# Routing's small SBUF operations move from VectorE to GpSimd in a fused attention and mixture-of-experts kernel

## The reference

```python
x = x + _L0_xcond_ref(_layernorm(x), ctx, ctx, lengths)      # 8 heads
x = x + _L0_ffn_ref(_layernorm(x), gate_w, w1, w2, w3)

scores = jnp.einsum('ti,ei->te', xt, gate_w)                 # 2048 tokens, 8 experts
probs = jax.nn.softmax(scores, axis=-1)
expert_weights, expert_indices = jax.lax.top_k(probs, 2)
expert_weights = expert_weights / expert_weights.sum(axis=-1, keepdims=True)
x1 = jax.nn.silu(jnp.einsum('ti,eoi->teo', xt, w1))          # 512 -> 1024
x3 = jnp.einsum('ti,eoi->teo', xt, w3)
expert_outs_all = jnp.einsum('teo,eio->tei', x1 * x3, w2)    # 1024 -> 512
```

## Time and profile before

| | us |
|---|---|
| median of three runs | 1231.14 (1230.88 to 1231.62) |
| the profiled execution | 1232.27 |
| its span, first to last instruction | 1230.7 |
| POOL's prep of slot 2 to prep of slot 13 | 331.50 |
| mean granted TensorE clock | 0.951 |

### The profile page before, as it was taken

One profiled execution on the slowest core, in us unless ns is written; L12 is line 12 of the kernel. 1 busy time (PEld: TensorE's weight loads), 2 busy tenths in 40 slices (PEclk: granted clock), 3 DMA queues, 4 the chain that ended last, 5 costly groups with the idle time before them and its releaser, 6 DMA issues.

```text
span 1230.7 us, 19877 instructions
## 1 busy us (share of the span) xinstructions
PE 1035.8 (84%) x5081; PEld 413.9 (34%) x5082; DVE 810.9 (66%) x953; ACT 410.7 (33%) x734; POOL 638.4 (52%) x578
## 2 busy tenths in 40 slices
PE   1799988999998998832999999999999999999910
PEld 0123322333333333211444444444444444444400
DVE  5877877888888887213853954938677395953354
ACT  3266666666666676721111111111100111011100
POOL 6454766676767762322841834807566182830055
PEclk9699999999999999975999999999999999999965
DMA  6465655565555552105875756647666575753387
GB/s 175 153 223 150 186 153 175 174 189 181 175 177 181 179 150 70 48 27 161 203 141 143 185 132 171 171 96 212 153 197 176 147 191 149 191 133 86 71 227 257
DMA packets 212839, 195.58 MB, mean 159 GB/s; under 512 B 137376, under 2 KB 176288, under 8 KB 207392
## 3 DMA queue, kind: packets, MB, share of 16 engines
q1 hardware_dynamic: 198624, 123.80, 38.5%
q0 software_dynamic: 14176, 71.31, 17.7%
HBM read 111.44 MB, written 52.95 MB: 134 GB/s over the span
## 4 chain that ended last, share of the span: by engine, by line
PE 49%; POOL 20%; DMA 11%; issue 10%; DVE 7%; POOLq 2%; ACT 1%; SPq 1%; DVEq 0%
PE rows L1072 23%; PE heads_out L1072 12%; POOL W L423 7%; PE heads_out L989 4%; PE scores L976 4%; DVE nm L717 3%; PE rows L962 3%; DMA rb<-recips_dram 3%; POOL W L422 3%; DMA recips_dram<-rden 2%; DMA U<-wpack_dram 2%; POOL us L500 1%; POOL us L497 1%; PE misc L1039 1%; POOL U L422 1%
## 5 line engine op out<-in xcount | busy, mean ns | idle before, releaser
L1072 PE MATMUL rows<-W,U 128*128 (+1 forms) x1776 | 391.9, 381 | 23.6 <-DMA U<-stage 19.5
L717 DVE TENSOR_REDUCE nm<-rows 128x2 f32<-128x1024 f32 x256 | 304.2, 1216 | 61.2 <-PE rows L962 53.1
L598 ACT ACTIVATE W<-scores 128x512 f32<-128x512 f32 x512 | 283.9, 596 | 153.0 <-PE scores L976 151.7
L1072 PEld LDWEIGHTS rows<-W,U 128*128 128x128 bf16 x1776 | 174.3, 98 | 236.0 <-issue 30.4
L663 ACT ACTIVATE U<-rows 128x512 f32<-128x512 f32 x78 | 46.4, 597 | 520.3 <-PE rows L1072 511.5
L962 PE MATMUL rows<-W,U 96*128 96x512 bf16 x512 | 151.6, 400 | 71.0 <-DVE nm L717 43.6
L1072 PE MATMUL heads_out<-W,U 128*128 x888 | 199.4, 381 | 13.3 <-issue 10.6
L423 POOL TENSOR_TENSOR W<-U,W 128x2048 bf16<-128x2048 f32 x42 | 172.6, 4110 | 7.7 <-POOL W L422 7.7
L900 DVE TENSOR_TENSOR U<-rows,U 128x512 f32<-128x512 f32 x78 | 53.6, 687 | 183.6 <-ACT U L663 183.5
L976 PE MATMUL scores<-U,W 128*128 128x512 bf16 x512 | 168.1, 386 | 5.6 <-ACT W L598 4.7
L907 DVE TENSOR_TENSOR U<-U 128x512 bf16<-128x512 f32 x78 | 162.7, 2086 | 2.7
(11 more groups left out here) (146 smaller groups left out, 676.4 us busy)
## 6 DMA issues: line engine op xcount, KB each, us to landing
U<-wpack_dram POOLq DMA_DIRECT2D x42, 1024.0 KB, 5.8
parts_dram<-U SPq DMA_DIRECT2D x32, 384.0 KB, 3.9
U<-parts_dram SPq DMA_DIRECT2D x32, 384.0 KB, 3.9
W<-parts_dram SPq DMA_DIRECT2D x32, 384.0 KB, 5.0
stage<-slots_dram SPq DMA_DIRECT2D x39, 256.0 KB, 2.8
expert_out_dram<-U SPq DMA_DIRECT2D x39, 256.0 KB
parts_dram<-U SPq DMA_DIRECT2D x32, 256.0 KB, 4.0
stage<-wpack_dram POOLq DMA_DIRECT2D x12, 512.0 KB, 4.8
```

The lines of the kernel that those rows point to most:

```text
L598: s.activation(probs[:, w % 2, j, kk, :], sc[u % 2][:, :], ACT.Exp) \
L717: v.tensor_reduce(nm[:, bb.parity, 2 * k:2 * k + 2], p1[k % 2][:, :].rearrange("p (c k) -> p c k", c=2), AX_X, ALU.max, negate=True).then_ ...
L1072: ins = m.matmul(bank, part_of(s_part, k), W[:, bass.ds(at_w, 512)], start=(k == 0 and n == 0), stop=(k == n_chunks - 1 and n == 2))
```

## The change

DVE keeps three routing operations, those that read PSUM: the maximum and its index (L729, L731 before) and the sum of rank and first rows (L767 before). The others go to POOL in two groups, in steps of their own. Group A (six steps) stands between prep and the weight chunk: two copies, where the expert numbers now pass through a new tile `order_f`, a cast and a copy; two compares with a scalar column in place of one with a broadcast; the sum of the masks. Group B (six steps) stands between the keys and the scatters: the product; a sum over the eight experts as three halving additions in place of one reduction; the cast to `idx`; and the running sum of masks, now last. DVE waits before it overwrites `sorted8` or `place` until POOL has read the last ones, and the table operations wait for the last `idx_ready`.

```diff
@@ -16,7 +16,7 @@
 P = 128
 LOOP_FIRST, LOOP_LAST = 2, 6
 LEAD = 4
-ENGINE_STEPS = {"prep": 10, "keys": 4, "z": 4, "route_a": 6, "route_b": 5}
+ENGINE_STEPS = {"prep": 10, "keys": 4, "z": 4, "top": 2, "route_a": 6, "route_b": 6}
 
 
 class Batch:
@@ -149,6 +149,7 @@
         ltri = sb("ltri", [P, P], BF16)
         onesb = sb("onesb", [P, P], BF16)
         idx = sb("idx", [P, 2, 2], I32)
+        order_f = sb("order_f", [P, 2], F32)
 
         tio_i = sb("tio_i", [P, T + 1], I32)
         tio = sb("tio", [P, 2, T + 1], F32)
@@ -190,7 +191,7 @@
 
 
         names = """setup numbered consts rows_set gate_in len_in ln_ready sb_ready table_chain
-            prep_steps keys_steps first_keys z_steps route_a_steps route_b_steps queries_out keys_out
+            prep_steps keys_steps first_keys z_steps top_steps route_a_steps route_b_steps queries_out keys_out
             sums_out rec_out m_out den_in rec_in m_in cv_in p1_ready p1_used scores_ready exp_done pv_done
             og_ready vt_ps vt_ready u_ready us_ready t_ready x1_ready x1_kept zt_ps zt_ready
             gate_ready gate_used mask_ready rank_ready rank_used idx_ready rec_ready st1_steps
@@ -454,6 +455,23 @@
                     g.nop().then_inc(S["prep_done"], 1)
                     if b.within(-2, -2):
                         constants()
+                pv2 = b.plus(-2)
+                if pv2.within(0, B - 1):
+                    a_steps = Steps(hold, S["route_a_steps"], pv2.n, ENGINE_STEPS["route_a"])
+                    hold(S["gate_used"], b.n - 1)
+                    if pv2.within(1, B - 1):
+                        hold(S["rank_ready"], b.n - 2)
+                    two = experts2[:, bass.ds(pv2.n, 1), :].rearrange("p o a -> p (o a)")
+                    a_steps.step(g.tensor_copy(scores2[:, bass.ds(pv2.n, 1), :].rearrange("p o a -> p (o a)"),
+                                               sorted8[:, 0:2]))
+                    a_steps.step(g.tensor_copy(order_f[:, :], order8[:, 0:2]))
+                    a_steps.step(g.tensor_copy(two, order_f[:, :]))
+                    for a in range(2):
+                        a_steps.step(g.tensor_scalar(masks[:, a, :], numbers[:, :], order_f[:, a:a + 1], None,
+                                                     ALU.is_equal))
+                    a_steps.step(g.tensor_tensor(maskb[:, :], masks[:, 0, :], masks[:, 1, :], ALU.add))
+                    a_steps.end()
+                    g.nop().then_inc(S["mask_ready"], 1)
                 if b.within(1, 1):
                     for n in range(2):
                         pool.dma_start(stage[:, n, :], wpack[0, :, n * CH:(n + 1) * CH]).then_inc(w_in[n], 16)
@@ -477,9 +495,22 @@
                     high_low(st, pt[:, 3, :], None, cin[:, lb.parity, :], rest[:, :])
                     high_low(st, pt[:, 4, :], pt[:, 5, :], rest[:, :])
                     st.end()
-                pv2 = b.plus(-2)
                 if pv2.within(0, B - 1):
-                    hold(S["idx_ready"], b.n - 1)
+                    b_steps = Steps(hold, S["route_b_steps"], pv2.n, ENGINE_STEPS["route_b"])
+                    row = rows[:, bass.ds(pv2.n, 1), :].rearrange("p o a -> p (o a)")
+                    hold(S["rank_used"], b.n - 1)
+                    b_steps.step(g.tensor_tensor(place[:, 0:2, :], masks[:, :, :],
+                                                 place[:, 2, :].unsqueeze(1).to_broadcast([P, 2, E]), ALU.mult))
+                    for n in (4, 2):
+                        b_steps.step(g.tensor_tensor(place[:, 0:2, 0:n], place[:, 0:2, 0:n], place[:, 0:2, n:2 * n],
+                                                     ALU.add))
+                    b_steps.step(g.tensor_tensor(row.unsqueeze(2), place[:, 0:2, 0:1], place[:, 0:2, 1:2], ALU.add))
+                    if b.within(4, B + 1):
+                        hold(slots_out[pv2.parity], pv2.pair * 32)
+                    b_steps.step(g.tensor_copy(idx[:, b.parity, :], row))
+                    b_steps.step(g.tensor_tensor(mask_sum[:, :], mask_sum[:, :], maskb[:, :], ALU.add))
+                    b_steps.end()
+                    g.nop().then_inc(S["idx_ready"], 1)
                     for a in range(2):
                         pool.indirect_dma_start(
                             out=zs[:, :], out_offset=bass.IndirectOffsetOnAxis(ap=idx[:, b.parity, a:a + 1], axis=0),
@@ -722,25 +753,18 @@
                 maxima(range(0, 2))
                 if routes:
 
-                    a_steps = Steps(dve.wait_ge, S["route_a_steps"], pv2.n, ENGINE_STEPS["route_a"])
+                    tops = Steps(dve.wait_ge, S["top_steps"], pv2.n, ENGINE_STEPS["top"])
                     dve.wait_ge(S["gate_ready"], b.n - 1)
-                    two = experts2[:, bass.ds(pv2.n, 1), :].rearrange("p o a -> p (o a)")
+                    if pv2.within(1, B - 1):
+                        v.nop().then_inc(S["dve_held"], 1)
+                        dve.wait_ge(S["mask_ready"], b.n - 2)
                     v.nop().then_inc(S["dve_held"], 1)
-                    a_steps.step(v.max(sorted8[:, :], misc[:, 0:E]))
+                    tops.step(v.max(sorted8[:, :], misc[:, 0:E]))
                     v.nop().then_inc(S["dve_held"], 1)
-                    a_steps.step(v.max_index(order8[:, :], sorted8[:, :], misc[:, 0:E]))
+                    tops.step(v.max_index(order8[:, :], sorted8[:, :], misc[:, 0:E]))
+                    tops.end()
                     v.nop().then_inc(S["gate_used"], 1)
-                maxima(range(2, 3))
-                if routes:
-                    a_steps.step(v.tensor_copy(scores2[:, bass.ds(pv2.n, 1), :].rearrange("p o a -> p (o a)"),
-                                               sorted8[:, 0:2]))
-                    a_steps.step(v.tensor_copy(two, order8[:, 0:2]))
-                    a_steps.step(v.tensor_tensor(masks[:, :, :], numbers[:, :].unsqueeze(1).to_broadcast([P, 2, E]),
-                                                 two.unsqueeze(2).to_broadcast([P, 2, E]), ALU.is_equal))
-                    a_steps.step(v.tensor_tensor(maskb[:, :], masks[:, 0, :], masks[:, 1, :], ALU.add))
-                    a_steps.end()
-                    v.nop().then_inc(S["mask_ready"], 1)
-                maxima(range(3, 6))
+                maxima(range(2, 6))
                 lb = b.plus(3)
                 if lb.within(0, B - 1):
                     dve.wait_ge(loads[lb.parity], lb.pair * 32 + 32)
@@ -762,23 +786,14 @@
                 maxima(range(7, 8))
                 if routes:
 
-                    b_steps = Steps(dve.wait_ge, S["route_b_steps"], pv2.n, ENGINE_STEPS["route_b"])
                     dve.wait_ge(S["rank_ready"], b.n - 1)
-                    b_steps.step(v.tensor_tensor(place[:, 2, :], misc[:, 0:E], first_rows[:, :], ALU.add))
-                    v.nop().then_inc(S["rank_used"], 1)
-                    b_steps.step(v.tensor_tensor(mask_sum[:, :], mask_sum[:, :], maskb[:, :], ALU.add))
-                    b_steps.step(v.tensor_tensor(place[:, 0:2, :], masks[:, :, :],
-                                                 place[:, 2, :].unsqueeze(1).to_broadcast([P, 2, E]), ALU.mult))
+                    if pv2.within(1, B - 1):
+                        v.nop().then_inc(S["dve_held"], 1)
+                        dve.wait_ge(S["idx_ready"], b.n - 2)
+                    v.nop().then_inc(S["dve_held"], 1)
+                    v.tensor_tensor(place[:, 2, :], misc[:, 0:E], first_rows[:, :], ALU.add) \
+                        .then_inc(S["rank_used"], 1)
                 maxima(range(8, 9))
-                if routes:
-                    row = rows[:, bass.ds(pv2.n, 1), :].rearrange("p o a -> p (o a)")
-                    b_steps.step(v.tensor_reduce(row, place[:, 0:2, :], AX_X, ALU.add))
-                    if b.within(4, B + 1):
-                        dve.wait_ge(slots_out[pv2.parity], pv2.pair * 32)
-                    v.nop().then_inc(S["dve_held"], 1)
-                    b_steps.step(v.tensor_copy(idx[:, b.parity, :], row))
-                    b_steps.end()
-                    v.nop().then_inc(S["idx_ready"], 1)
                 maxima(range(9, 10))
                 if b.within(-3, -3):
 
@@ -828,6 +843,8 @@
             st = Steps(dve.wait_ge, S["table_chain"], 1, 7)
             link = st.step
             dve.wait_ge(S["pv_done"], 4 * B)
+            v.nop().then_inc(S["dve_held"], 1)
+            dve.wait_ge(S["idx_ready"], B)
             link(v.tensor_tensor(gexp[:, :].unsqueeze(2), scores2[:, :, 1:2], scores2[:, :, 0:1], ALU.subtract))
             v.nop().then_inc(S["routed"], 1)
             chosen = experts2[:, :, :].rearrange("p b a -> p (b a)").unsqueeze(2)
```

## The result

The changed kernel takes **1285.32 us** (median of 4 runs, 1283.95 to 1287.34), against 1231.38 (1230.88 to 1240.61) for the kernel before on the same chip. The ratio is 1.0432, 95% interval 1.0401 to 1.0463: 54 us slower. The profiled execution took 1285.01, its span is 1283.6, which is 52.9 more than before.

What follows compares the result with a forecast made beforehand. The prediction took POOL's chain of small dependent operations as the bound in slots 2 to 12. Its terms, 63.8 - 10.9 + 3.7 = +56.6 us, gave 1288.9 on the profiled execution, 1288 against the median; range 1270 to 1308.

Steps and rivals of the forecast that it cites:

- POOL is the period of slots 2 to 12: Attention phase, slots 2 to 12: POOL's chain of small dependent operations sets the 30.1 us slot; PE and DVE follow.
- 5.8 us a slot: Time both groups add to POOL's chain per slot, 2.95 plus 2.85; 63.8 us over slots 2 to 12.
- The `rb` cover of 10.9: Slots 2 to 12: POOL's 10.9 us of waits for the DMA of `rb` all go, leaving +52.9.
- Slots 13 to 16: POOL's slack or idleness hides the added work: 0; at worst +3 in slot 13, +0.5 each in 14 to 16.
- Slot 17: Last slot, nothing hides the groups in its chain: +2.1 for group A, +1.6 for group B, +3.7 together.
- Expert phase 0: Expert phase: none of its instructions changes, so its time changes by 0.
- PE's wait for the mask: Before PE's rank product: group A just ends in time (247.95 against 248.20); a longer wait costs nothing, with 5.8 us spare.
- The first, DVE's relief: Rival, slots 2 to 12: PE and DVE set the period, so relieving DVE makes it faster, 1213 us; chance 0.02.
- The second, the clock: Rival, each slot: PE pauses some 5 us, its clock falls and PE becomes the bound, 1315 us; chance 0.08.
- The third: Rival, slots 2 to 12: the 16.7 us DVE round trip absorbs POOL's work or steps overlap, 1271 us; chance 0.06.

Runs made afterwards that it cites:

- The twelve copies: Kernel before, all routing left on DVE, with POOL repeating both groups' twelve operations on scratch tiles nobody reads: 1284.97 us.
- (10): Kernel before with two DMAs moved, lighter POOL (ACT makes the chunk's high part, prep subtracts the mean directly) and group A on POOL: 1224.92 us.
- B alone: Kernel before with only group B moved to POOL, group A staying on DVE: 1260.99 us.
- A alone: Kernel before with only group A moved to POOL, group B staying on DVE: 1255.02 us.
- (6): Kernel before with SP sending the reciprocals ahead of the key and query reload, and POOL issuing the next chunk's transfer behind z: 1218.64 us.
- (4): Kernel before with the means subtracted directly in prep and z, and the weight chunk's high part made by ACT: 1257.29 us.

## Why the prediction came out as it did

Forecast 1288 in 1270 to 1308; measured 1285.32. By its own steps:

- **POOL is the period of slots 2 to 12: shown.** The twelve copies, with DVE and PE left as they were, give the whole loss.
- **5.8 us a slot: 5.47.** Group A was 2.95 and measured 3.06. A copy or addition takes 0.18 to 0.20, and from one step's start to the next are 0.35 to 0.54, around the 0.40 assumed; the two comparisons with a scalar column take 0.31 to 0.32. Group B was 2.85 and measured 2.55: its steps stand 0.43 apart (2.14 us from the first to the sixth), so that the waits and slices put at 0.45 cost next to nothing. The Trainium skill's factor of two for two-input elementwise work ("GPSIMD Engine Reference", Engine selection) does not show here: L472 takes 0.20, the same addition on DVE 0.17. At this size the wait between two steps costs as much as the step.
- **The `rb` cover of 10.9 goes: 10.6 did.** So the slots gave 60.2 - 10.6 = +49.6 where +52.9 was forecast.
- **Slots 13 to 16 cost nothing: wrong by 4.6.** The term of slot 13 said "0", "at worst +3 if PE comes late itself", and that of slots 14 to 16 "0, at worst +0.5 each". PE did come late. Its clock is 0.67 in the first 5.5 us of slot 14, as the pause in slot 13 left it, and PE starts the transposes of z 2.5 us after z's end (527.01 against 524.48), where it was 0.7 before (475.61 against 474.95). In slot 14 PE is busy 27.65 of 29.73 us; POOL isn't the bound there, so the lost clock shows in full: +3.0, with +1.4 in slot 13. Two other traces bear this out: with the copies and with the change and its DMAs moved slot 14 begins at a granted clock of 1.00, and it takes 27.0 and 27.3 us, near the 26.7 of before. I had judged the clock only where POOL covers it.
- **Slot 17: +3.7 forecast, +3.7 measured**, group A +1.7 instead of +2.1, group B +1.65 as said, 0.4 in the handing over.
- **Expert phase 0:** it came 3.5 shorter, within its own scatter. It and the start (-1.5) offset the term of slots 13 and 14: 49.6 + 4.6 + 3.7 - 1.5 - 3.5 = 52.9.
- **PE's wait for the mask costs nothing:** group A ended at 261.21, the rank product began at 263.52.

**Rivals.** The first, DVE's relief, is refuted by the copies; where POOL has room (10), relief of DVE and group A on POOL together are worth 0.3 us a slot. The second, the clock, was right in its first half: a pause of 2.0 to 5.7 us in each slot, then a lower clock, 0.91 over the slots. The price was 2.2 us of PE's time a slot, near the 1.7 of rows 12, and fits under 5.8. The Trainium skill's warning ("TensorE: Matmul & The Clock Gate", HAM oscillation) agrees with the trace as to the fall, once a slot; its cost appears where POOL isn't behind, in slots 13 and 14, and perhaps in B alone. The third needed the round trip over L826 and L832 to absorb work; it stayed at 16.7.

The forecast thus held by its mechanism, with a slot's price 6% too high and a missing term of about the same size.

Left open: late `rb` and the low clock go together in B alone, and an early `rb` removes the waits and 13.3 us of these slots but not the low clock, so the loop from clock to `rb` is argued and not shown. Nor is it shown why A alone, with the larger addition, has no late `rb`. The traces have a hint: group A stands ahead of the chunk's transfer, which in slots 2 to 11 of A alone leaves 0.7 to 3.7 us after the store of the reciprocals, and `rb`'s load follows that store by 4.2 to 4.7 us; in B alone the transfer leaves ahead of the store in nine of these ten slots, by up to 3.6 us, and the load follows by 4.9 to 6.3. No run moved the transfer alone.

## What to carry to other kernels

Ask of each engine how long its chain of dependent steps is in one round of the loop, not how busy it is: POOL at 69% was the period, and twelve operations of 0.2 us cost 5.5 us because each brings its semaphore wait. Moving small work off a busy engine is free only if the receiver has waits for others in that very stretch, and a round trip that it waits out is none; here, even with such waits, the move gained nothing (10). First look at what the bounding engine does wait for: two DMAs issued in another order gave 15 us where the move lost 54.

## What the runs showed of the hardware

- POOL's 128x512 operation with two scalar columns took 0.77 us as add and multiply and 2.08 as subtract and multiply. A comparison with a scalar column over 8 columns took 0.31 to 0.32, a copy or addition 0.18 to 0.20.
- A small store followed by a dependent load took longer behind other transfers. Over slots 2 to 12 `rb`'s load came 1.6 to 2.0 us after the store of the reciprocals when that went first (6), 4.4 to 6.4 behind the reload (before, where a chunk's transfer leaves within 0.6 us of the store), 3.9 to 7.5 where the chunk's transfer leaves 1.8 to 4.3 us ahead of it (4). The Trainium skill ("DMA: Bandwidth & Descriptors", Queues, rings and completion order) has a rule that would give this: a completion's semaphore write lands only after every earlier write of the same DMA engine, on whatever queue. The three orders agree with it; they don't prove it, since shared bandwidth would also slow the store.
- After a pause of PE the granted clock was 0.50 for 2 to 6 us: in every slot 2 to 12 of the change (pauses of 2.0 to 5.7 us), in none of before (longest wait for the maxima 2.3 us). B alone's executions spread over 14 us, A alone's over 1; with `rb` early B's spread over 4.
